# The stores of finished blocks are issued from ScalarE's queue in place of SyncE's, in a two-layer LoRA kernel on one core

## The chip, the core and the metric

The kernel runs on one core of a Trainium2 chip. The metric is the device time of one launch in microseconds (us), the median of several launches. A core has a matrix engine (TensorE, PE in the profile), three engines that work on tiles (VectorE or DVE, ScalarE or ACT, GpSimd or POOL) and SyncE (SP), which here only starts transfers. ScalarE starts some transfers too. Each engine runs its own instructions in the order in which they are written, and waits at semaphores for the others. A transfer, once issued, is carried out by 16 DMA engines, which all issuers share. The profile names SyncE's queue of transfers q1, and ScalarE's q10.

## What is computed

Two layers follow each other, each with a residual and a low-rank adapter that is picked per batch entry from a list of ids:

```python
def _L0_cond_ref(x, adapter_ids, base_weight, base_bias, lora_A_w, lora_B_w):
    result = jnp.einsum('bsd,od->bso', x, base_weight) + base_bias
    A = lora_A_w[adapter_ids]
    Bw = lora_B_w[adapter_ids]
    h = jnp.einsum('bsd,brd->bsr', x, A)
    return result + jnp.einsum('bsr,bor->bso', h, Bw)
...
def _L1_cond_ref(x, adapter_mapping, W, b, lora_As, lora_Bs):
    base_out = jnp.einsum('bti,oi->bto', x, W) + b
    A = lora_As[adapter_mapping]
    Bm = lora_Bs[adapter_mapping]
    lora_h = jnp.einsum('bti,bir->btr', x, A)
    return base_out + jnp.einsum('btr,bro->bto', lora_h, Bm) * 2
...
x = x + _L0_cond_ref(x, itok_B_6_15, ...)
x = x + _L1_cond_ref(x, itok_B_0_23, ...)
```

`x` has 8 batch entries of 512 tokens with 2048 features, float32. Both weights are 2048 x 2048, the adapters have rank 16, and there are 32 of each.

## The kernel before

The two weights are merged on the chip into one: C' (`wc_t` in HBM) is the product of the two layers' weights with their residuals, so that each token goes through one large product. The main loop has 6 planes (`pl`). Planes 0 and 1 (`pl < PRE`) make the two halves of C' out of `v_t` (the first weight, transposed) and the second weight; planes 2 to 5 take two batch entries each through C' and write `out_t`.

Each plane is one product of 2 x 2 blocks in Strassen's form: 7 products, run in the order M5, M3, M2, M4, M1, M7, M6. Four of them (M5, M2, M1, M6) need a sum or difference of two weight blocks. Each product has 16 steps; `g` counts the steps, 672 in all. A step takes one piece of weights of 128 x 512 values, `w_raw`, through these stations:

- SP loads it (`load_w`, L574), 6 steps ahead; the load waits until VectorE has finished with the piece four steps before (L571).
- For a product with a summed weight, ScalarE's queue loads the second piece, `w_second` (`load_second`, L974), 5 steps ahead, and POOL adds the two (L830). There are three buffers for `w_second`.
- ScalarE makes the high part `w_hi` (`w_split_hi`, L899), two steps ahead. It waits until TensorE has finished the step three before, since `w_hi` has three buffers (`RING`).
- VectorE makes the low part `w_lo` (L1073).
- TensorE runs 12 products of 128 x 512 (L1551 to L1553: high by high, low by high, high by low, four times).

The activations of a product go through the same split into `xop_hi` (ScalarE, L912) and `xop_lo` (VectorE, L1098), behind a sum on VectorE (L1088) where two blocks are added. After two steps an accumulator is full, and VectorE adds it into one or two blocks of the plane's result `c_out` (`evict`, L1239 and L1242); each such update counts the semaphore `c_updated` up. In planes 2 to 5 a small adapter product per accumulator goes before that (`up`; its operand `b_raw` is loaded by SP at L625 and split by ScalarE at L937). In planes 0 and 1 VectorE also adds products with the bias (`c_acc`, L1179), and adapter rows go out to HBM and back through `q_half` (SP L655 and L644, VectorE L1156).

A block of the result gets its last update in M3, M4, M7 or M6. The function `store(q, m)` then waits for that update and writes 256 KB of `c_out` out: to `wc_t` in planes 0 and 1 (L667, 64 stores), to `out_t` in planes 2 to 5 (L670, 128 stores). At step `g` those stores are issued whose evictions VectorE runs at step `g - 2`. `evictions(g)` lists them: in M7 and M6 they fall in pairs of neighbouring steps with two free steps between.

SP's program at one step is, in this order: `load_w(g + 6)`, loads of the next plane's `x_in` (L579 and L582, in M3, M7 and M6), `b_raw`, adapter rows, `q_half`, and the stores. ScalarE's is: `w_split_hi(g + 2)`, `load_second(g + 5)`, the high parts of activations, `h_split`, `b_split` and `a_split`.

Of the kernel before, what the change touches and what calls it, by code (L numbers as in the profile page):

```python
# [27 lines left out]
NPROD = len(PRODUCTS)  # L28
# [23 lines left out]
def two_layer_lora_kernel(nc, x_t, ids0, ids1, w0_t, w1_t, bias0, bias1,  # L52
# [10 lines left out]
    MH = MT // 2  # L63
# [30 lines left out]
    def upd_count(q, m, u):  # L94

        pl, i = divmod(q, NPROD)
        return pl * UPD_PASS + UPD_BASE[i] + m * N_UPD[i] + u + 1
# [20 lines left out]
    def evictions(g):  # L118

        q, j = divmod(g, STEPS)  # L120
        out = []
        for late in (1, 0):
            if 0 <= q - late < NQ:
                out += [(q - late, m) for m in EVICT.get(((q - late) % NPROD, j, late), [])]
        return out
# [98 lines left out]
    with ctx:  # L224
# [182 lines left out]
        def block_no(half, th):  # L407
            return half * 2 + th
# [18 lines left out]
        def c_diag_count(blk, m):  # L427

            return ((0, 1), (0, 0), (1, 0), (1, 1)).index(blk) * TT + m % TT + 1
# [83 lines left out]
        def columns_of(w_t, pl, th, tile):  # L513

            b = 2 * pl + th
            return w_t[TT * b:TT * b + TT, :, tile * P:(tile + 1) * P].rearrange("o p n -> p o n")

        def as_tiles(ap):
            return ap.rearrange("p (o n) -> p o n", o=TT)

        @block.sync
        def _(sp):
# [131 lines left out]
                    dst = pb_t[2 if diff else pl, :, 0:RANK, col:col + T // 2]  # L654
                sp.dma_start(dst, q_half[:, :]).then_inc(p_stored, 16)  # L655

            def store(q, m):
                pl, i = divmod(q, NPROD)
                for u, (blk, _) in enumerate(PRODUCTS[i][5]):
                    if FINAL[blk] == (i, u):  # L660
                        oh, th = blk
                        b = block_no(oh, th)
                        sp.wait_ge(c_updated, upd_count(q, m, u))
                        if pl < PRE:
                            if oh == pl and m // TT == th:
                                sp.wait_ge(c_diag_done, c_diag_count(blk, m))
                            sp.dma_start(columns_of(wc_t, pl, th, oh * MH + m), as_tiles(c_out[:, b, m, :])  # L667
                                         ).then_inc(out_stored[b], 16)
                        else:
                            sp.dma_start(out_t[2 * (pl - PRE) + th, oh * MH + m, :, :], c_out[:, b, m, :]  # L670
                                         ).then_inc(out_stored[b], 16)


            for l, ids_d in enumerate((ids0, ids1)):
                sp.dma_start(ids[0:1, l, :], ids_d.rearrange("(o n) -> o n", o=1)).then_inc(ids_loaded, 16)
# [33 lines left out]
            for g in range(NG):  # L709
                q, j = divmod(g, STEPS)  # L710
                pl, i = divmod(q, NPROD)
                s = g + 6

                for n in PARTS_AT.get(g - 1, [])[2 if g == 0 else 0:]:
                    if n + PIN < NPART:
                        load_part(n + PIN)
                    store_part(n)
                if STEPS <= s < NG:
                    load_w(s)

                if g == 0:
                    sp.wait_ge(v_stored[1], NU // 2 * 16)
                if g < 2:
                    for k in range(4 * g, 4 * g + 4):
                        load_x(0, 0, 1, k)
                if g == 2:
                    sp.dma_start(q_t[:, :], q_rows[:, :]).then_inc(small_stored, 16)
                    sp.dma_start(qd_t[:, :], qd_rows[:, :]).then_inc(small_stored, 16)
                    sp.dma_start(pb_t[2, :, RANK:R2, :], b1d_rows[:, :]).then_inc(small_stored, 16)
                if q == M1 and j < BATCH:  # L730
                    sp.dma_start(pb_t[0:2, j, RANK:R2, :].rearrange("h r n -> r h n"),
                                 lora_b1[bass.ds(adapter_of(1, j), 1), :, :].rearrange("o r (h n) -> (o r) h n", h=2)
                                 ).then_inc(b1_stored, 16)
                if g == 4:
                    sp.wait_ge(h_bias_stored, 16)
                    sp.wait_ge(h_bias_zero, 1)
                    for quad in (0, 2, 3):
                        sp.dma_start(h_bias[quad * R2 + RANK:(quad + 1) * R2, :],
                                     hb_t.rearrange("(b r) -> r b", r=RANK),
                                     allow_slow_non_contiguous=True).then_inc(h_bias_loaded, 16)  # L740
                if q == M3 and j < 2:
                    sp.wait_ge(part_filled, 2 * NPART)
                    for k in range(4 * j, 4 * j + 4):
                        load_x(0, 0, 0, k)
                if q == M3 and j == 8:
                    sp.wait_ge(ag_added, GROUPS)
                    sp.dma_start(ag_t.rearrange("b p n -> p b n"), ag[:, :, :, :].rearrange("p b k r -> p b (k r)")
                                 ).then_inc(ag_stored, 16)
                if q == M3 and 8 <= j < 12:
                    for k in range(2 * (j - 8), 2 * (j - 8) + 2):  # L750
                        load_x(0, 1, 0, k)


                if pl + 1 < NPL and i in (M7, M6) and j == 2:
                    sp.wait_ge(x_summed, n_sums(q) + KH)
                    if pl < PRE:
                        sp.wait_ge(c_scaled, (pl * 2 + (1 if i == M7 else 2)) * KT)
                if pl + 1 < NPL and i == M7 and j >= 2 and (j % 2 == 0 or j == 15):
                    load_x(pl + 1, 1, 1, (j - 1) // 2)
                if pl + 1 < NPL and i == M6:  # L760
                    for n in range(2 * KH):
                        if j == 2 + n * 14 // 16:
                            load_x(pl + 1, 0, 1 - n // KH, n % KH)
                if pl > 0 and i == M3 and j % 2 == 0:
                    load_x(pl, 1, 0, j // 2)
                for b in b_units_at(g, B_LOAD_AT):
                    load_b(*b)
                if (v := a_unit_at(g + 4)) is not None:
                    if v < PRE * 4:
                        load_a_pre(v)  # L770
                    elif v % 2 == 0:
                        load_a(v // 2)
                if (e := p_add_at(g, 1)) is not None:
                    store_p(*e)
                if (e := p_add_at(g, -2)) is not None:
                    load_q(*e)
                if g >= 2:
                    for qq, m in evictions(g - 2):
                        store(qq, m)
            for g in range(NG, NG + 4):  # L780
                for qq, m in evictions(g - 2):
                    store(qq, m)
            for qq, m in evictions(NG + 2):
                store(qq, m)
            for b in range(4):
                sp.wait_ge(out_stored[b], NPL * MH * 16)

# [46 lines left out]
        def _(act_e):  # L834
# [105 lines left out]
            def h_split_hi(pl, th):  # L940
# [4 lines left out]
                else:  # L945
# [3 lines left out]
                nc.scalar.activation(h_split[:, th, :], h_acc[:, :], ACT.Identity,  # L949
                                     bias=h_bias[:, b:b + 1]).then_inc(h_hi_ready, 1)  # L950

            def load_second(s):

                if not (STEPS <= s < NG and is_sum_w(s)):
                    return
                q, j = divmod(s, STEPS)
                pl, i = divmod(q, NPROD)
                m, h = ORDER[j]
                oh, dh = PRODUCTS[i][1][1]
                n = second_no(s)  # L960
                if s == M2 * STEPS:
                    for i_v in range(2):
                        act_e.wait_ge(v_stored[i_v], NU * 16 // 2)
                    for i_v in range(PRAW):
                        act_e.wait_ge(part_stored[i_v], NPART // PRAW * 16)
                if pl == PRE and j == 0 and i in (M5, M2):
                    for b in range(4):
                        act_e.wait_ge(out_stored[b], (PRE if i == M2 else 1) * MH * 16)
                if n >= RAW2:
                    act_e.wait_ge(w_summed, STEPS + n - RAW2 + 1)  # L970
                else:
                    act_e.wait_ge(g_turned, GROUPS)
                col = (dh * KH + h * KS) * P
                act_e.dma_start(w_second[:, n % RAW2, :], w_source(pl)[oh * MH + m, :, col:col + SW]  # L974
                                ).then_inc(wb_loaded[n % RAW2], 16)
# [50 lines left out]
            for g in range(NG):  # L1026
                q, j = divmod(g, STEPS)
                pl, i = divmod(q, NPROD)
                if g + 2 < NG:
                    w_split_hi(g + 2)  # L1030
                load_second(g + 2 + RAW2)
                for n in PART_ENDS:
                    if PART_G_AT[n] == g:
                        copy_part_g(n)
# [20 lines left out]
                    b_split_hi(*b)  # L1055
                if (v := a_unit_at(g)) is not None:
                    a_split_hi(v)

        @block.vector
        def _(dve):  # L1060
# [551 lines left out]
```

## Time and profile before

| | |
|---|---|
| time, median of 3 launches | 2151.89 us (2150.59 to 2154.97) |
| time of the profiled launch | 2147.73 us |
| its span (first to last instruction) | 2146.0 us |
| TensorE busy | 2075.3 us (97%) |
| VectorE busy | 1567.4 us (73%) |
| ScalarE busy | 737.5 us (34%) |
| GpSimd busy | 693.3 us (32%) |
| DMA queues, share of 16 engines | q1 (SP) 51.1%, q10 (ScalarE) 18.9% |
| bytes moved | 459.08 MB, mean 214 GB/s |

The profile shows one launch. Its own time is 4.2 us under the median of the three launches, and 1.7 us above its span. A busy TensorE is not the same as one at its peak, since its products are pipelined and overlap in the records. Issuing a transfer isn't counted as busy time of an engine. "Landing" is the time from a transfer's issue to its completion.

### The profile page before, as it was taken

The page shows a single profiled execution, that of the slowest core. Times are in us where ns is not written, and L with a number is a line of the kernel's source. Part 1 is how long each engine was busy: PE and PEld are TensorE (multiplying, and loading weights), DVE is VectorE, ACT ScalarE, POOL GpSimd, SP SyncE. Part 2 cuts the span into 40 slices and gives each one's busy share as a digit, 9 for nine tenths or more (in the row PEclk, how much of TensorE's full clock was granted, in tenths as well). Part 3 has the DMA queues.
Part 4 walks back from the last instruction along what each step waited for, and adds up shares of the span by engine and source line. Part 5 has one row for each costly group of instructions (what it writes and reads, how often), then busy time and mean ns, then how long its engine had stood idle before and what let it go on. Part 6 is the DMA issues. An engine that isn't in the chain of part 4 may idle for free.

```text
span 2146.0 us, 27823 instructions
## 1 busy us (share of the span) xinstructions
PE 2075.3 (97%) x9340; PEld 1710.8 (80%) x9340; DVE 1567.4 (73%) x2165; ACT 737.5 (34%) x1302; POOL 693.3 (32%) x498
## 2 busy tenths in 40 slices
PE   5799899999999999999999999999999999999999
PEld 5687787778788877888888888887888888888887
DVE  3557767977886887676876676876676876767875
ACT  5553222223322323333333333333333333333332
POOL 0222313444121445041545140544230445221443
PEclk9899999999999999999999999999999999999999
DMA  9975837796655698564698574789574789574676
GB/s 269 292 244 156 254 115 235 213 298 219 200 168 165 207 276 277 149 209 140 208 290 292 147 222 125 216 263 304 151 218 120 215 256 319 160 220 121 211 219 194
DMA packets 320122, 459.08 MB, mean 214 GB/s; under 512 B 27884, under 2 KB 131308, under 8 KB 319468
## 3 DMA queue, kind: packets, MB, share of 16 engines
q1 hardware_dynamic: 252908, 334.59, 51.1%
q10 hardware_dynamic: 67072, 122.71, 18.9%
q8 instruction: 75, 1.23, 0.2%
q14 instruction: 67, 0.55, 0.1%
HBM read 383.80 MB, written 74.45 MB: 214 GB/s over the span
## 4 chain that ended last, share of the span: by engine, by line
PE 73%; DVE 12%; DMA 8%; issue 3%; ACT 2%; SPq 1%; POOL 1%; ACTq 0%; DVEq 0%; POOLq 0%
PE acc L1551 22%; PE acc L1553 21%; PE acc L1552 21%; DVE w_lo L1073 4%; DMA w_raw<-wc_t 2%; DVE xop_lo L1098 2%; DVE c_out L1242 2%; DVE c_acc L1179 2%; PE h_acc L1463 2%; PE h_acc L1459 2%; DVE x_sum L1088 2%; DMA w_raw<-v_t 1%; PE acc L1473 1%; POOL w_raw L830 1%; DMA b_raw<-pb_t 1%
## 5 line engine op out<-in xcount | busy, mean ns | idle before, releaser
L1551 PE MATMUL acc<-xop_hi,w_hi 128*128 128x512 f32 x2688 | 1058.8, 394 | 29.8 <-DVE w_lo L1073 26.0
L830 POOL TENSOR_TENSOR w_raw<-w_raw,w_second 128x512 f32<-128x512 f32 x464 | 654.7, 1413 | 1268.5 <-DMA w_second<-wc_t 526.1
L1553 PE MATMUL acc<-xop_lo,w_hi 128*128 128x512 f32 x2688 | 1049.1, 390 | 0.0
L1552 PE MATMUL acc<-xop_hi,w_lo 128*128 128x512 f32 x2688 | 1049.0, 390 | 0.0
L1073 DVE TENSOR_TENSOR w_lo<-w_raw,w_hi 128x512 fp32r<-128x512 f32 x672 | 583.0, 871 | 406.3 <-ACT w_hi L899 402.8
L899 ACT ACTIVATE w_hi<-w_raw 128x512 fp32r<-128x512 f32 x672 | 423.9, 631 | 1181.9 <-PE acc L1553 1009.3
L1551 PEld LDWEIGHTS acc<-xop_hi,w_hi 128*128 128x128 f32 x2688 | 506.2, 188 | 151.9 <-DVE w_lo L1073 43.7
L1553 PEld LDWEIGHTS acc<-xop_lo,w_hi 128*128 128x128 f32 x2688 | 506.0, 188 | 106.2
L1552 PEld LDWEIGHTS acc<-xop_hi,w_lo 128*128 128x128 f32 x2688 | 506.4, 188 | 101.9
L1088 DVE TENSOR_TENSOR x_sum<-x_in 128x512 f32<-128x512 f32 x240 | 214.2, 904 | 0.1
L1242 DVE TENSOR_TENSOR c_out<-acc,c_out 128x512 f32<-128x512 f32 x304 | 202.2, 682 | 7.8 <-PE acc L1473 6.2
L1098 DVE TENSOR_TENSOR xop_lo<-x_sum,xop_hi 128x512 fp32r<-128x512 f32 x240 | 156.2, 682 | 4.7 <-ACT xop_hi L912 4.1
L912 ACT ACTIVATE xop_hi<-x_sum 128x512 fp32r<-128x512 f32 x240 | 135.2, 589 | 50.3 <-DVE x_sum L1088 46.8
L1098 DVE TENSOR_TENSOR xop_lo<-x_in,xop_hi 128x512 fp32r<-128x512 f32 x96 | 91.9, 990 | 0.1
L1136 DVE SCALAR_TENSOR_TENSOR b_split<-b_raw,b_split 32x128 fp32r<-32x128 f32 x128 | 51.5, 402 | 40.4 <-ACT b_split L937 37.1
L1459 PE MATMUL h_acc<-xop_hi,a_split 128*128 128x512 f32 x192 | 74.8, 390 | 0.0
L1463 PE MATMUL h_acc<-xop_lo,a_split 128*128 128x512 f32 x192 | 74.8, 389 | 0.0
L1239 DVE SCALAR_TENSOR_TENSOR c_out<-acc,c_bias,x_in 128x512 f32<-128x512 f32 x96 | 71.3, 743 | 0.0
L814 POOL TENSOR_TENSOR w_raw<-v_part 128x512 f32<-128x512 f32 x16 | 23.5, 1491 | 131.7 <-ACT v_part L873 66.6
L937 ACT ACTIVATE b_split<-b_raw 128x128 fp32r<-128x128 f32 x128 | 38.7, 302 | 73.9 <-DMA b_raw<-pb_t 72.7
L1179 DVE SCALAR_TENSOR_TENSOR c_acc<-x_in,bias,c_acc 128x512 f32<-128x512 f32 x64 | 60.1, 940 | 0.1
L912 ACT ACTIVATE xop_hi<-x_in 128x512 fp32r<-128x512 f32 x96 | 55.5, 616 | 6.0 <-DMA hb_t<-e_raw 6.0
(116 smaller groups left out, 839.4 us busy)
## 6 DMA issues: line engine op xcount, KB each, us to landing
w_raw<-wc_t SPq DMA_DIRECT2D x448, 256.0 KB, 3.8
w_second<-wc_t ACTq DMA_DIRECT2D x320, 256.0 KB, 4.4
w_raw<-v_t SPq DMA_DIRECT2D x208, 256.0 KB, 4.0
w_second<-v_t ACTq DMA_DIRECT2D x144, 256.0 KB, 4.3
x_in<-x_t SPq DMA_DIRECT2D x128, 256.0 KB, 6.1
out_t<-c_out SPq DMA_DIRECT2D x128, 256.0 KB, 5.3
x_in<-w_t SPq DMA_DIRECT2D x64, 256.0 KB, 5.6
wc_t<-c_out SPq DMA_DIRECT2D x64, 256.0 KB, 5.4
```

Of the source, the lines that this page charges most:

```text
L830: nc.gpsimd.tensor_tensor(w_raw[:, r, :], w_raw[:, r, :], w_second[:, n % RAW2, :], ALU.add if sign > 0 else ALU.subtract).then_inc(w_summ ...
L899: nc.scalar.activation(flat(w_hi[:, s % RING, :, :]), w_raw[:, r, :], ACT.Copy).then_inc(w_hi_ready, 1)
L912: nc.scalar.activation(xop_hi[:, n % XRING, :], src, ACT.Copy).then_inc(x_hi_ready, 1)
L1073: nc.vector.tensor_tensor(flat(w_lo[:, s % RING, :, :]), w_raw[:, s % RAW, :], f(flat(w_hi[:, s % RING, :, :])), ALU.subtract).then_inc(w_ ...
L1088: nc.vector.tensor_tensor(x_sum[x_bank(ns)][:, :], x_tile(q, 0, k), x_tile(q, 1, k), ALU.add if sign > 0 else ALU.subtract).then_inc(x_sum ...
L1098: nc.vector.tensor_tensor(xop_lo[:, n % XRING, :], src, f(xop_hi[:, n % XRING, :]), ALU.subtract).then_inc(x_lo_ready, 1)
L1242: nc.vector.tensor_tensor(c, bank[:, :], old, ALU.add).then_inc(c_updated, 1)
L1459: nc.tensor.matmul(h_acc[:, :], cols, xop_hi[:, n % XRING, :], start=(k == 0 and which == 0), stop=False)
L1463: mm = nc.tensor.matmul(h_acc[:, :], cols, xop_lo[:, n % XRING, :], start=False, stop=end)
L1551: nc.tensor.matmul(bank[:, :], wh, xh, start=(k == 0), stop=False)
L1552: nc.tensor.matmul(bank[:, :], wl, xh, start=False, stop=False)
L1553: mm = nc.tensor.matmul(bank[:, :], wh, xl, start=False, stop=end)
```

## The change

The function `store` moves from SyncE's block to ScalarE's, with its wait for `c_updated` (and in planes 0 and 1 for `c_diag_done`). Its calls stand on ScalarE right behind `w_split_hi(g + 2)` and `load_second(g + 5)` of the same step, ahead of everything else ScalarE does in the step. What is stored, and in which order, stays the same; SP still waits at the end for all stores.

```diff
@@ block.sync
-                if g >= 2:
-                    for qq, m in evictions(g - 2):
-                        store(qq, m)
-            for g in range(NG, NG + 4):
-                for qq, m in evictions(g - 2):
-                    store(qq, m)
-            for qq, m in evictions(NG + 2):
-                store(qq, m)
             for b in range(4):
                 sp.wait_ge(out_stored[b], NPL * MH * 16)
@@ block.scalar
+            def store(q, m):
+                pl, i = divmod(q, NPROD)
+                for u, (blk, _) in enumerate(PRODUCTS[i][5]):
+                    if FINAL[blk] == (i, u):
+                        oh, th = blk
+                        b = block_no(oh, th)
+                        act_e.wait_ge(c_updated, upd_count(q, m, u))
+                        if pl < PRE:
+                            if oh == pl and m // TT == th:
+                                act_e.wait_ge(c_diag_done, c_diag_count(blk, m))
+                            act_e.dma_start(columns_of(wc_t, pl, th, oh * MH + m), as_tiles(c_out[:, b, m, :])
+                                         ).then_inc(out_stored[b], 16)
+                        else:
+                            act_e.dma_start(out_t[2 * (pl - PRE) + th, oh * MH + m, :, :], c_out[:, b, m, :]
+                                         ).then_inc(out_stored[b], 16)
...
                 if g + 2 < NG:
                     w_split_hi(g + 2)
                 load_second(g + 2 + RAW2)
+                if g >= 2:
+                    for qq, m in evictions(g - 2):
+                        store(qq, m)
...
+            for g in range(NG, NG + 5):
+                for qq, m in evictions(g - 2):
+                    store(qq, m)
```

Three places show how the instructions now stand. The first is ScalarE's queue in M6 of plane 2, the last product of the first plane that writes outputs. Before, a high part and a second load make a step, with small splits behind them:

```order
L899 ACTIVATE w_hi<-w_raw 128x512
L974 DMA w_second<-wc_t 128x512
L937 ACTIVATE b_split<-b_raw 128x128
L899 ACTIVATE w_hi<-w_raw 128x512
L974 DMA w_second<-wc_t 128x512
L912 ACTIVATE xop_hi<-x_in 128x512
L899 ACTIVATE w_hi<-w_raw 128x512
L974 DMA w_second<-wc_t 128x512
```

In the changed kernel the same stretch reads:

```order
L875 ACTIVATE w_hi<-w_raw 128x512
L966 DMA w_second<-wc_t 128x512
L941 DMA out_t<-c_out 128x512
L913 ACTIVATE b_split<-b_raw 128x128
L875 ACTIVATE w_hi<-w_raw 128x512
L966 DMA w_second<-wc_t 128x512
L941 DMA out_t<-c_out 128x512
L888 ACTIVATE xop_hi<-x_in 128x512
L875 ACTIVATE w_hi<-w_raw 128x512
L966 DMA w_second<-wc_t 128x512
```

Two stores in neighbouring steps now stand between second loads, and ahead of the splits of `b_raw` and `x_in`.

The second place is SP's queue in the same product. Before:

```order
L574 DMA w_raw<-wc_t 128x512
L582 DMA x_in<-x_t 128x512
L625 DMA b_raw<-pb_t 128x1x128
L670 DMA out_t<-c_out 128x512
L574 DMA w_raw<-wc_t 128x512
L582 DMA x_in<-x_t 128x512
L625 DMA b_raw<-pb_t 128x1x128
L670 DMA out_t<-c_out 128x512
L574 DMA w_raw<-wc_t 128x512
L582 DMA x_in<-x_t 128x512
```

And in the changed kernel:

```order
L574 DMA w_raw<-wc_t 128x512
L582 DMA x_in<-x_t 128x512
L625 DMA b_raw<-pb_t 128x1x128
L574 DMA w_raw<-wc_t 128x512
L582 DMA x_in<-x_t 128x512
L625 DMA b_raw<-pb_t 128x1x128
L574 DMA w_raw<-wc_t 128x512
L582 DMA x_in<-x_t 128x512
```

The loads of weights, activations and `b_raw` stand as before, without the stores between them.

The third place is ScalarE's queue in M3 of plane 0, where the first four stores of the program fall. Before:

```order
L899 ACTIVATE w_hi<-w_raw 128x512 x2
L921 ACTIVATE a_split<-b_half_51 128x1024
L899 ACTIVATE w_hi<-w_raw 128x512 x3
L974 DMA w_second<-v_t 128x512
L899 ACTIVATE w_hi<-w_raw 128x512
L974 DMA w_second<-v_t 128x512
```

And in the changed kernel:

```order
L875 ACTIVATE w_hi<-w_raw 128x512 x2
L938 DMA wc_t<-c_out 128x4x128
L897 ACTIVATE a_split<-b_half_51 128x1024
L875 ACTIVATE w_hi<-w_raw 128x512
L938 DMA wc_t<-c_out 128x4x128
L875 ACTIVATE w_hi<-w_raw 128x512 x2
L966 DMA w_second<-v_t 128x512
L938 DMA wc_t<-c_out 128x4x128
L875 ACTIVATE w_hi<-w_raw 128x512
L966 DMA w_second<-v_t 128x512
```

The first two stores stand behind the high parts of steps 26 and 27, and the third behind the first load of a second piece.

## Rows read from the trace of the kernel before

**Rows 1.** Waits, whole span: who waited for whom, us, times, longest.
```profile
ACT w_hi L899 <- PE acc L1553: 1009.3, 514, 6.5
PE acc L1551 <- DVE w_lo L1073: 26.0, 24, 5.5
```

**Rows 2.** Waits of SP's queue, whole span.
```profile
SPq L574 <- DVE w_lo L1073: 1306.5, 556, 7.1
```

**Rows 3.** Instructions by line: durations of an issue in ns, min/median/max.
```profile
L974 ACTq DMA_DIRECT2D w_second<-wc_t x320: 326/326/365, 812.6 to 2125.6; - x160
L670 SPq DMA_DIRECT2D out_t<-c_out x128: 332/475/1632, 903.0 to 2143.5; - x128
L667 SPq DMA_DIRECT2D wc_t<-c_out x64: 370/438/1859, 219.4 to 838.8; - x64
```

**Rows 4.** Timeline at the longest wait for an eviction: start us, us, engine.
```profile
241.81 0.63 ACT L899 ACTIVATE w_hi<-w_raw 128x512 fp32r<-128x512 f32 x1
248.95 0.63 ACT L899 ACTIVATE w_hi<-w_raw 128x512 fp32r<-128x512 f32 x1 [6.51 <-PE acc L1553]
...
245.48 0.68 DVE L1242 TENSOR_TENSOR c_out<-acc,c_out 128x512 f32<-128x512 f32 x1
```

**Rows 5.** Timeline where high parts of activations follow the store.
```profile
584.69 1.14 ACT L912 ACTIVATE xop_hi<-x_in 128x512 fp32r<-128x512 f32 x2
586.87 0.63 ACT L899 ACTIVATE w_hi<-w_raw 128x512 fp32r<-128x512 f32 x1 [1.04 <-PE acc L1553]
...
585.74 0.68 DVE L1242 TENSOR_TENSOR c_out<-acc,c_out 128x512 f32<-128x512 f32 x1
```

**Rows 6.** Timeline of TensorE behind two of its longest waits.
```profile
243.74 0.79 PE L1551 MATMUL acc<-xop_hi,w_hi 128*128 128x512 f32 x1 [5.47 <-DVE w_lo L1073]
...
1469.15 0.50 PE L1551 MATMUL acc<-xop_hi,w_hi 128*128 128x512 f32 x1 [1.51 <-DVE w_lo L1073]
```

**Rows 7.** Chain that ended last, 205 to 250 us: start us, us, what.
```profile
228.15 6.51 DMA pb_t<-q_half
...
234.68 4.36 DMA q_half<-qd_t
```

**Rows 8.** Stretches: length, busy us (instructions) of PE PEld DVE ACT POOL, PEclk, DMA share, GB/s.
```profile
214.00:217.00 3.00, 3.00 (x15) 2.49 (x14) 3.00 (x5) 0.00 (x0) 0.00 (x0) 1.00 0.48 131
...
223.00:226.00 3.00, 3.00 (x15) 2.50 (x14) 3.00 (x6) 0.63 (x1) 0.00 (x0) 1.00 1.10 315
...
244.00:248.00 4.00, 4.00 (x10) 3.13 (x11) 3.97 (x7) 0.00 (x0) 1.13 (x1) 0.50 0.62 181
```

**Rows 9.** Timeline of DVE, ACT and SP around the first store.
```profile
211.90 0.68 DVE L1242 TENSOR_TENSOR c_out<-acc,c_out 128x512 f32<-128x512 f32 x1
...
213.02 0.63 ACT L899 ACTIVATE w_hi<-w_raw 128x512 fp32r<-128x512 f32 x1 [2.37 <-PE acc L1553]
...
219.44 1.47 SPq L667 DMA_DIRECT2D wc_t<-c_out  x1
```

**Rows 10.** Stretch in M6 of plane 2, columns as in rows 8.
```profile
1117.00:1160.00 43.00, 42.89 (x189) 35.21 (x189) 26.70 (x36) 16.02 (x31) 19.89 (x15) 1.00 0.99 335
```

**Rows 11.** Landings of `w_second` (L974) issued 1117 to 1163 us.
```profile
DMA to landing us min/median/max: 3.3/6.0/7.5
```

**Rows 12.** Landings of `w_raw` (L574) issued 1117 to 1163 us.
```profile
DMA to landing us min/median/max: 3.9/7.1/9.7
```

**Rows 13.** Landings of `out_t` (L670) issued 1117 to 1163 us.
```profile
DMA to landing us min/median/max: 6.3/6.7/9.0
```

**Rows 14.** Waits in 1117 to 1163 us.
```profile
ACT w_hi L899 <- POOL w_raw L830: 13.5, 7, 2.6
POOL w_raw L830 <- DMA w_raw<-wc_t: 13.3, 7, 3.5
...
POOL w_raw L830 <- DMA w_second<-wc_t: 9.8, 6, 2.8
```

More of the change, by code:

```diff
@@ L655, in store_p @@
                 sp.dma_start(dst, q_half[:, :]).then_inc(p_stored, 16)
[L657 to L671, printed above, removed]
             for l, ids_d in enumerate((ids0, ids1)):
```

## The prediction

> **What bounds the kernel now.** I read four views, from the whole to the place. First the waits of the whole span: ScalarE waits 1009.3 us for TensorE, and TensorE waits 26.0 us, in 24 pieces, for low parts of weights [rows 1]. With TensorE busy in 97% of the span, TensorE is the bound, and what any change of queues can give back is those 26.0 us and what they cost in clock. Second, SP's own waits: it stands 1306.5 us before loads of `w_raw`, waiting for VectorE [rows 2]. SP's queue is thus far from full on the average, and its time is worth something only in stretches where it falls behind. Third, the longest of TensorE's waits: 5.47 us at 243.74 us, in M3 to M2 of plane 0, and as an example of the others 1.51 us at 1469.15 us [rows 6]. Fourth, the DMA share by stretch: it is 1.10 around 225 us and 0.99 in M6 of plane 2, where the loads for the next plane run [rows 8, 10]. There the DMA engines are the scarce thing, and an issuer can only change the order in which they are used.
>
> **What the change takes from SP.** The 192 issues have medians of 475 ns (128 of them) and 438 ns (64) [rows 3]: 128 x 0.475 + 64 x 0.438 = 89 us leave SP's queue. SP has 1306.5 us of waiting to set against that, so outside the saturated stretches the gain is 0. `w_raw` is issued when VectorE releases it, with or without stores in front.
>
> **What it adds to ScalarE: issue time.** An issue of `w_second` takes ScalarE's queue 326 ns [rows 3]. The nearest row for a store there is that one from below and SP's 475 ns from above, so 63 to 91 us go into a queue that waits 1009.3 us for TensorE. Cost 0. The cover would be gone only where ScalarE has no wait before its next high part. I take the lower value, since SP's longer issues stand in stretches where its own queue of transfers is full.
>
> **What it adds to ScalarE: a wait.** The store of step g waits for an eviction that VectorE makes in its step g - 2. Behind it on ScalarE stand the step's high parts of activations, `b_split`, `a_split`, and the next step's high part of weights and load of a second piece. The worst place is in M3 of plane 0: the high part starts at 241.81 us and ends at 242.44, the eviction ends at 245.48 + 0.68 = 246.16 us, and the next high part starts only at 248.95 us, behind TensorE [rows 4]. The wait of 3.7 us fits into that gap with 2.8 us to spare. The worst place with work right behind is in M3 of plane 1: two high parts of activations start at 584.69, the first update ends at 585.74 + 0.68 = 586.42 [rows 5]. They start 586.42 + 0.33 - 584.69 = 2.1 us late, take 1.14 us, and move the next high part from 586.87 to about 587.9, by 1.0 us. VectorE needs none of these before it has done its steps g - 1 and g, since the eviction waited for belongs to g - 2. Where VectorE is late enough to make ScalarE wait, it is also late in asking for ScalarE's work. Cost 0. From above: the few places with such work right behind, three of this kind at 1.0 us, give 3 us.
>
> **M3 of plane 0.** This is the dearest wait of the kernel. TensorE stands 5.47 us [rows 6], and afterwards runs at a granted clock of 0.50, that is 1.2 in place of 2.4 GHz: 10 products in 4.00 us [rows 8], where 43.00 / 189 = 0.2275 us each [rows 10] would give 17.6. That is 7.6 x 0.2275 = 1.7 us more, 7.2 us in all. The chain to it goes through SP's queue: `q_half` is stored at 228.15 us, lands 6.51 us later, is loaded again at 234.68 and lands after 4.36 us [rows 7]. In this stretch SP issues without a pause, the store at 219.44 takes it 1.47 us [rows 9], and the first two stores of C' stand ahead of the adapter row. Is that row now earlier? The first store can go much sooner. Its eviction ends at 211.90 + 0.68 = 212.58 us, ScalarE's high part ends at 213.65, so it goes at about 213.7 in place of 219.44 [rows 9], into a stretch with a DMA share of 0.48 [rows 8]. But the third and fourth are also no longer held back by SP, and fall into the stretch with share 1.10, beside the row that matters. About as many bytes as before come before it. I take 0. From below the whole 7.2 us come back; from above one store more ahead costs what one issue under back-pressure took, 1.5 us, with its share of slow clock 2 us.
>
> **M6 of planes 0 to 4.** Here second pieces are loaded for M6 and M5, the next plane's activations come in, and stores follow in pairs. A store of 256 KB is now in the queue of `w_second`, between two of them. In M6 of plane 2 `w_second` lands in 6.0 us, `w_raw` in 7.1, `out_t` in 6.7 (medians) [rows 11, 12, 13]. POOL waits for `w_raw` 7 times (13.3 us) and for `w_second` 6 times (9.8 us), and ScalarE 13.5 us for POOL [rows 14]: both are at the edge. There is a ring: the high part of step s is made beside the issue of the second piece of s + 3, so a landing that grows by d makes each third step later by d. If `w_second` lands like the stores, d = 0.7, and 16 steps give 0.7 x 16 / 3 = 3.7 us. The lead of ScalarE over TensorE is two steps, 2 x 12 x 0.2275 = 5.5 us; less a high part of 0.63 [rows 4] and about as much for the low part, 4.1 us are left to eat. So TensorE pays 0 at d = 0.7. `w_raw`, without stores in its queue, may be sooner by as much, on the 7 waits that it ends. I take 0.2 us for each of the five, +1 us, since the lead is not whole when M6 begins. Bounds: -1 (POOL's waits for `w_raw` shorten) and +1.8 each (below).
>
> The Trainium skill speaks against a gain here: its page "DMA: Bandwidth & Descriptors", section "Issuing engines are not separate DMA queues", says that transfers started by several engines run on the same 16 DMA engines and interleave, so that only the issue time is saved. The trace agrees in part: in the saturated stretch both queues are slow, 6.0 and 7.1 us, though not alike. By the rule alone the sum would be 0 in place of +1.
>
> **The end.** The last stores go out from one idle queue in place of another: 0.
>
> **The sum.** 0 + 0 + 0 + 0 + 1 + 0 = +1 us on 2147.7 us for the profiled launch. That launch is 4.2 us under the median of the three, so on the median I have 2151.9 + 1 = 2153 us. Within 0.2% (4.3 us) is about what a measurement of this kernel can't tell from no change.
>
> **The rivals.**
>
> *The stall in M3 goes* (faster). If the early first store and the shorter SP queue bring the adapter row forward, VectorE isn't held and 7.2 us come back; `w_raw` and `b_raw` sooner in M6 would take the wait at 1469.15 us too, 1.5 us. Together 8.7: 2143 us. For it: SP's issue of 1.47 us shows a queue of transfers that is full. Against: DMA shares of 1.10 leave nothing to win by order except for who comes first. Chance 0.22.
>
> *Second pieces come late* (slower). It decides from d = 4.1 x 3 / 16 = 0.8 us on. If `w_second` becomes as slow as `w_raw` now is, d = 7.1 - 6.0 = 1.1, 16 steps give 5.9 us, less 4.1 of lead 1.8 us in each of five planes, 9 us: 2161 us. For it: in M6 the issues of `w_second` are already close to the point where POOL waits. Against: the DMA engines' total work is the same, and a later product pulls its loads apart. Chance 0.26. A rule of the Trainium skill would bring this about: the same page, section "Queues, rings and completion order", has each DMA engine take turns between the rows of its queues, packet by packet. A short queue would then keep its turn only as long as it is short, and each store delays the second piece behind it. No row here shows the turns themselves.
>
> *ScalarE's wait isn't hidden* (slower). The three places of M3 with high parts behind the store pay in full, 3 us, and a wait of TensorE of 5.47 us has shown that the clock then adds a third: +4 and the +1 of above, 2157 us. Against: the ordering argument above. Chance 0.06.
>
> *No part of it shows*: the likeliest, with its own range 2148 to 2156. Chance 0.46.
>
> **How the numbers follow.** The predicted time is that of the likeliest case, 2153 us. Faster 0.22 is the first rival, slower 0.32 the second and third. The range of 2144 to 2163 us reaches to the fast rival's better half and takes in most of the slow one.
>
> **What would show it.** Right: DMA issues of `w_second` near 0.33 us with stores beside them; SP's wait before `w_raw` longer by some 80 us; TensorE's wait for low parts near 26 us in all; a wait near 243 us of 4 to 7 us. In M6 `w_second` should land in 6.5 to 7 us and `w_raw` in 6 to 7. Wrong: no half-clock stretch near 245 us (the fast rival), POOL's waits for `w_second` well up and TensorE waiting in M6 of planes 2 to 4 (the slow one), or high parts that start right behind an eviction with TensorE waiting (the third).

## The result

The changed kernel takes 2155.12 us (median of 20 launches, 2144.24 to 2166.27), the kernel before 2148.26 us (20 launches, 2139.57 to 2154.97). The ratio is 1.0033, with a 95% interval of 1.002 to 1.0046. It is slower by 0.33%, some 7 us; the forecast was 2153 us, with "No part of it shows" as the likeliest case. The measured time lies in the stated range, but the loss came by a way that none of the rivals named.

The profiled launch of the changed kernel took 2163.83 us and is near the top of its spread, while that of the kernel before lies at its median. So of the 16 us between the two profiles less than half is the change. Page of the changed kernel, its DMA queues, and who waited for whom (us in total, times, longest):

```profile
q1 hardware_dynamic: 200684, 284.25, 43.9%
q10 hardware_dynamic: 119296, 173.06, 25.8%
```

```profile
ACT w_hi L875 <- PE acc L1551: 930.9, 477, 5.8
...
ACT b_split L913 <- DMA b_raw<-pb_t: 110.7, 57, 5.4
...
PE acc L1549 <- DVE w_lo L1071: 38.6, 25, 5.0
```

SP's own waits:

```profile
SPq L574 <- DVE w_lo L1071: 1435.0, 583, 8.7
```

Seven percent of the DMA engines' time went from SyncE's queue to ScalarE's. SP stands 128 us longer before its loads of `w_raw` (1306.5 us before [rows 2]), more than the 89 us of issues that left it. ScalarE waits less for TensorE (1009.3 us before [rows 1]), and TensorE more for low parts, 38.6 in place of 26.0 us. The row for which the prediction has no term is the second: ScalarE waits 110.7 us for `b_raw`, which the prediction names only in its fast rival, as coming sooner. In the kernel before that row reads:

```profile
ACT b_split L937 <- DMA b_raw<-pb_t: 72.7, 51, 4.0
```

TensorE's longest wait in the changed kernel is still the one near 244 us, 4.97 us. The next three (start us, us) stand in M6 of planes 2, 3 and 4, where the longest of the kernel before is the 1.51 us at 1469.15 us [rows 6]:

```profile
1142.05 0.50 PE L1549 MATMUL acc<-xop_hi,w_hi 128*128 128x512 f32 x1 [4.29 <-DVE w_lo L1071]
...
1476.24 0.50 PE L1549 MATMUL acc<-xop_hi,w_hi 128*128 128x512 f32 x1 [4.01 <-DVE w_lo L1071]
...
1811.76 0.58 PE L1549 MATMUL acc<-xop_hi,w_hi 128*128 128x512 f32 x1 [3.48 <-DVE w_lo L1071]
```

The chain of work that TensorE waited for (start us, us), led back from the third of them, holds four loads of `b_raw`, 35 of its last 54 us:

```profile
1757.55 10.20 DMA b_raw<-pb_t
...
1770.51 8.64 DMA b_raw<-pb_t
...
1785.66 5.72 DMA b_raw<-pb_t
...
1795.44 10.42 DMA b_raw<-pb_t
...
1805.88 0.32 ACT b_split L913
...
1806.55 1.43 DVE a_raw L1112
1808.00 0.43 DVE a_raw L1115
...
1810.43 0.68 DVE c_out L1240
1811.11 0.61 DVE w_lo L1071
```

Each load waits until VectorE has split an earlier one, since `b_raw` has two buffers. ScalarE's timeline shows what stands behind such a split:

```profile
1800.30 0.63 ACT L875 ACTIVATE w_hi<-w_raw 128x512 fp32r<-128x512 f32 x1 [2.27 <-POOL w_raw L806]
...
1805.88 0.31 ACT L913 ACTIVATE b_split<-b_raw 128x128 fp32r<-128x128 f32 x1 [4.95 <-DMA b_raw<-pb_t]
1808.54 0.63 ACT L905 ACTIVATE a_split<-a_raw 128x512 fp32r<-128x512 f32 x1 [2.34 <-DVE a_raw L1115]
...
1809.59 0.61 ACT L875 ACTIVATE w_hi<-w_raw 128x512 fp32r<-128x512 f32 x1
```

The next high part of weights is written behind the split, and comes 9.3 us after the last one, where a step is 2.7 us long. The late load makes 4.95 us of that. Most of the rest is other work of the same step: it is step 8 of M6, in which VectorE also sums the adapter operand `a_raw` behind its part of `b_split`, and ScalarE splits it (`a_split`) ahead of the next high part. VectorE then has its part of `a_split`, an eviction and the low part to do. The waits of 4.29 and 4.01 us have the same chain behind them, with loads of `b_raw` of 9.06 and 9.93 us and the same `a_split`. So a late `b_raw` hurts most where this second split stands behind it; no run moved `a_split`. The two steps of lead are gone, TensorE waits 3.48 us, and then runs slowly for a while (stretch, busy us and instructions of PE PEld DVE ACT POOL, granted clock, DMA share, GB/s):

```profile
1812.00:1815.00 3.00, 3.00 (x8) 2.34 (x8) 2.97 (x4) 0.21 (x1) 1.40 (x1) 0.51 0.93 240
```

The granted clock is 0.51, the lower of its two levels (1.2 GHz). Eight products in 3.00 us, where 0.2275 us each would give 13, cost 1.2 us more.

The profiled launch is a slow one, but e1 and e5 below, profiled at 2154.22 and 2155.47 us, close to their medians, have such waits in M6 of planes 2, 3 and 4 too: 2.60, 4.15 and 2.66 us in e1, 2.86, 1.03 and 4.23 us in e5.

### The profile page after: what moved, and what is told of

Its sections match the earlier page's. It is cut to its first block, busy times and chain, and to the rows that moved or that the text cites. A ratio compares the mean times of both kernels' runs of the same rounds, so it can differ in the third digit from the quotient of the medians.

```text
span 2162.1 us, 27823 instructions
## 1 busy us (share of the span) xinstructions
PE 2078.3 (96%) x9340; PEld 1714.2 (79%) x9340; DVE 1574.9 (73%) x2165; ACT 740.7 (34%) x1302; POOL 690.3 (32%) x498
## 4 chain that ended last, share of the span: by engine, by line
PE 74%; DVE 11%; DMA 8%; issue 3%; ACT 1%; SPq 1%; POOL 1%; ACTq 0%; DVEq 0%; POOLq 0%
PE acc L1549 22%; PE acc L1551 22%; PE acc L1550 22%; DVE w_lo L1071 3%; DMA b_raw<-pb_t 3%; PE h_acc L1461 2%; PE h_acc L1457 2%; DVE c_out L1240 2%; DVE xop_lo L1096 2%; DVE x_sum L1086 2%; DVE c_acc L1177 1%; DMA w_raw<-v_t 1%; PE acc L1471 1%; DMA v_t<-v_raw 1%; DMA q_half<-pd_t 1%
## 5 line engine op out<-in xcount | busy, mean ns | idle before, releaser
L1549 PE MATMUL acc<-xop_hi,w_hi 128*128 128x512 f32 x2688 | 1059.0, 394 | 42.1 <-DVE w_lo L1071 38.6
L1071 DVE TENSOR_TENSOR w_lo<-w_raw,w_hi 128x512 fp32r<-128x512 f32 x672 | 589.3, 880 | 380.5 <-ACT w_hi L875 377.2
L1086 DVE TENSOR_TENSOR x_sum<-x_in 128x512 f32<-128x512 f32 x240 | 222.6, 939 | 0.1
L1096 DVE TENSOR_TENSOR xop_lo<-x_in,xop_hi 128x512 fp32r<-128x512 f32 x96 | 82.7, 892 | 2.3 <-ACT xop_hi L888 2.1
L913 ACT ACTIVATE b_split<-b_raw 128x128 fp32r<-128x128 f32 x128 | 39.0, 305 | 118.4 <-DMA b_raw<-pb_t 110.7
```

The source lines that it names most:

```text
L1071: nc.vector.tensor_tensor(flat(w_lo[:, s % RING, :, :]), w_raw[:, s % RAW, :], f(flat(w_hi[:, s % RING, :, :])), ALU.subtract).then_inc(w_ ...
L1086: nc.vector.tensor_tensor(x_sum[x_bank(ns)][:, :], x_tile(q, 0, k), x_tile(q, 1, k), ALU.add if sign > 0 else ALU.subtract).then_inc(x_sum ...
L1096: nc.vector.tensor_tensor(xop_lo[:, n % XRING, :], src, f(xop_hi[:, n % XRING, :]), ALU.subtract).then_inc(x_lo_ready, 1)
L1549: nc.tensor.matmul(bank[:, :], wh, xh, start=(k == 0), stop=False)
```

## The experiments

Three theories were set against each other. **T**: transfers. Stores that no longer stand behind SyncE's loads are carried out ahead of them, SyncE's loads land later, and `b_raw` with its two buffers is the one that TensorE feels. **R1**: ScalarE's order. ScalarE stands at stores whose eviction isn't done. **R2**: weights. `w_second` or `w_raw` lands late, and POOL is the one that is waited for (the slow rival of the prediction). Each kernel was timed against the kernel before in five rounds, with 12 launches (the changed kernel 20); all ratios are to the kernel before as timed beside it. The last column is from the one profiled launch of each, and TensorE feels only part of it.

| kernel | ratio | 95% interval | median us | wait of ScalarE for `b_raw`, us |
|---|---|---|---|---|
| changed kernel | 1.0033 | 1.002 to 1.0046 | 2155.12 | 110.7 |
| e1: only M7 and M6 moved | 1.003 | 1.0011 to 1.005 | 2156.12 | 99.3 |
| e2: only M3 and M4 moved | 1.0002 | 0.9989 to 1.0015 | 2151.73 | 90.9 |
| e3: changed, `b_raw` early | 0.9976 | 0.9958 to 0.9995 | 2146.31 | 26.5 |
| e4: before, `b_raw` early | 1.0003 | 0.9988 to 1.0018 | 2150.69 | 21.6 |
| e5: changed, stores two steps later | 1.0027 | 1.001 to 1.0044 | 2155.42 | 70.8 |
| e6: changed, `b_raw` on ScalarE | 0.9994 | 0.997 to 1.0018 | 2149.01 | 4.1 |
| e7: changed, `b_raw` first in the step | 1.0008 | 0.9989 to 1.0028 | 2151.22 | 9.3 |
| e8: e3, adapter rows first | 0.9968 | 0.9949 to 0.9987 | 2143.18 | 19.0 |
| e9: before, stores first in the step | 1.0023 | 1.0008 to 1.0037 | 2152.86 | 80.7 |
| e10: e4, adapter rows first | 0.9998 | 0.9981 to 1.0015 | 2146.92 | 21.9 |
| e11: e8, stores one step later | 0.9995 | 0.9981 to 1.0009 | 2146.65 | 28.4 |
| e12: e3 again | 0.9975 | 0.9959 to 0.9991 | 2143.78 | 18.9 |

### Where: e1 and e2

```diff
 # ScalarE, behind load_second; SyncE issues the others as before
                 if g >= 2:
                     for qq, m in evictions(g - 2):
+                        if qq % NPROD in (M7, M6):     # e2: (M3, M4)
                         store(qq, m)
```

Expected of e1: 

> Only the stores of M7 and M6 are issued by ScalarE, those of M3 and M4 by SyncE as before. Theory (T): the loss comes where stores and the next plane's loads share the DMA engines, and the stores now overtake SyncE's loads of weights and b_raw. Then this kernel loses all of the 0.33%: 2154 to 2157 us against 2148. Rival (R1): ScalarE's wait for late evictions costs, wherever the eviction is late, above all behind M3 and M4, where it ends after the high part at most planes. Then this kernel loses a third or less: within 3 us of before.

Expected of e2: 

> Only the stores of M3 and M4 are issued by ScalarE. (T): no load of activations runs there in planes 2 to 5, so it is as before, within 3 us of 2148, and the wait of 5.5 us in M3 of plane 0 may be a little shorter. (R1): most of the 7 us is lost here.

e1 loses what the whole change loses (1.003), e2 nothing (1.0002). The loss is made by the stores of M7 and M6, where the next plane's activations are loaded. R1, which had the late evictions behind M3 and M4, fails its first test. e2's wait for `b_raw` of 90.9 us in its profiled launch warns that this sum alone does not set the time: what counts is where the waits stand.

### What carries it: e3, e4 and e12

```diff
-M7: (-3, -2, 1, 2, 5, 6, 9, 10)}          # B_LOAD_AT
+M7: (-4, -3, -1, 0, 3, 5, 7, 9)}
+        def b_buf(bu):
+            return ident[:, :] if bu % 3 == 2 else b_raw[:, bu % 3, :]
...
-                if bu >= 2:
-                    sp.wait_ge(b_lo_ready, bu - 1)
-                sp.dma_start(b_raw[:, bu % 2, :],
...
+                if bu >= 3:
+                    sp.wait_ge(b_lo_ready, bu - 2)
+                sp.dma_start(b_buf(bu),
```

Expected of e3: 

> The changed kernel with a third buffer for b_raw, and its loads for M7 and M6 one or two steps earlier. (T) with b_raw as the carrier of the loss: ScalarE's wait for b_raw falls from 110.7 us to under 40, TensorE's waits of 3.5 to 4.3 us in M6 of planes 2 to 4 go, and the time falls by 5 to 12 us against the changed kernel, to 2144 to 2150. Rival (R2): weights are the carrier, w_raw lands late and POOL waits for it; then the waits in M6 stay, and the time is within 3 us of 2155.

Expected of e4: 

> The kernel before with the same third buffer and the same earlier loads of b_raw: the control of the run above. (T): ScalarE waits 72.7 us for b_raw before, and little of it reaches TensorE, so 0 to 5 us faster than 2148; the gap between the two stores' places shrinks from 7 us to under 3. (R2): gap of 7 us as before.

Expected of e12: 

> The changed kernel with the third buffer of b_raw and its earlier loads, the same kernel as e3, run again beside fresh runs of the kernel before. It was 0.9976 (0.9958 to 0.9995), and a near relative with stores one step later was 0.9995. If the gain over the kernel before is real, the ratio is again 0.995 to 0.999 and clear of 1; if it was the luck of one chip and hour, it is within 0.1% of 1. Either way it should stay clear of the changed kernel's 1.0033.

The third buffer is `ident`, an identity matrix that isn't read any more in planes 2 to 5. With a third buffer and earlier loads the changed kernel loses its 0.33% and is faster than the kernel before, 0.9976, and 0.9975 when run again. The same edit on the kernel before is worth nothing (1.0003). R2 is out as the carrier of this loss: if POOL's waits for weights had made the loss, a third `b_raw` would not have taken it away. The waits in M6 of plane 4, first those of the changed kernel (1762 to 1821 us), then those of e3 (1748 to 1802 us):

```profile
POOL w_raw L806 <- DMA w_raw<-wc_t: 24.0, 12, 4.3
ACT b_split L913 <- DMA b_raw<-pb_t: 20.8, 7, 5.2
DVE b_split L1134 <- ACT b_split L913: 14.4, 6, 4.6
...
PE acc L1549 <- DVE w_lo L1071: 5.2, 3, 3.5
```

```profile
POOL w_raw L813 <- DMA w_raw<-wc_t: 19.2, 10, 3.6
...
PE acc L1556 <- DVE w_lo L1078: 0.4, 1, 0.4
```

The waits for `b_raw` are gone and TensorE's with them, though POOL still waits 19.2 us for `w_raw`: those waits are hidden. The two launches compared are a slow and a fast one (2163.83 and 2141.12 us), so the times above, and not these rows, carry the argument. The edit gives a buffer and moves loads at once; which of the two does it wasn't tested. I had expected the gap between the two places of the stores to shrink; it turned round, which the theory didn't foresee.

### Not ScalarE's order: e5

```diff
-                if g >= 2:
-                    for qq, m in evictions(g - 2):
+                if g >= 4:
+                    for qq, m in evictions(g - 4):
                         store(qq, m)
```

Expected of e5: 

> The changed kernel with its stores issued four steps behind the eviction in place of two, so that ScalarE never waits for an eviction; nothing else moves. Theory (T): the loss comes from transfers, since stores in a queue of their own are served beside SyncE's loads and hold b_raw up. Later stores hold it up as much: 2152 to 2158 us against 2149 to 2152. Rival (R1): ScalarE stands at stores whose eviction isn't done, and what is behind it (b_split, high parts) comes late. Then the whole loss goes: within 2 us of before.

With two steps more between eviction and store, ScalarE's waits that end with VectorE's updates of `c_out` fall from 13.6 to 5.2 us, and the kernel stays as slow as it was (1.0027). R1 is out. The sum of the waits for `b_raw` is as low as 70.8 us here, yet TensorE still waits 4.2 us at once in M6 of plane 4, and the rows there read (1757 to 1815 us):

```profile
ACT b_split L913 <- DMA b_raw<-pb_t: 11.1, 4, 3.5
PE acc L1549 <- DVE w_lo L1071: 4.2, 1, 4.2
```

### Order in the queues: e6, e7 and e9

```diff
 # e7, SyncE
+                for b in b_units_at(g, B_LOAD_AT):
+                    load_b(*b)
                 if STEPS <= s < NG:
                     load_w(s)
...
-                for b in b_units_at(g, B_LOAD_AT):
-                    load_b(*b)
```

e6 has the same two lines on ScalarE, between `load_second` and the stores. e9 is the kernel before with the stores at that place in SyncE's step.

Expected of e6: 

> The changed kernel with the loads of b_raw on ScalarE's queue too, behind the loads of second pieces and ahead of the stores; two buffers, same steps. (T): b_raw leaves the queue that holds w_raw and x_in, lands in 5 to 6 us in place of 7 to 8 in M7 and M6, and the loss is gone or turned: 2144 to 2150 us. (R1): the order of ScalarE's work gets longer by 128 issues and waits, so 2155 us or more. If b_raw lands no sooner, turn-taking between the queues isn't what held it up.

Expected of e7: 

> The changed kernel with SyncE's loads of b_raw ahead of the weights and activations of the same step, still in SyncE's queue. (T): two transfers of 256 KB no longer stand ahead of b_raw, each worth 0.7 to 1.3 us, so it lands 1.5 to 2.5 us sooner and most of the loss goes: 2146 to 2152 us. (R2, weights as carrier): no change, 2155 us.

Expected of e9: 

> The kernel before, all in SyncE's queue, with the stores at the head of SyncE's step, ahead of the weights, activations and b_raw of the same step. If what costs is that a store is served ahead of b_raw, in whatever queue, then the loss shows without any second queue: ScalarE's wait for b_raw rises from 72.7 us to 90 or more, and the time is 2152 to 2156 us against 2149. If it takes a second queue to overtake (turns between queues), one store of 0.7 us more ahead of b_raw is not enough: within 2 us of before, and the wait for b_raw under 85 us.

Putting `b_raw` ahead of two transfers of the same step takes the wait for it from 110.7 to 9.3 us, and most of the loss by the median (1.0008, though the interval reaches 1.0028). The small waits don't mean fast landings. In M6 of planes 2 to 4 TensorE still waits 1.84, 1.49 and 2.26 us, each at the step with `a_split`, and the chain of the last one holds this load:

```profile
1786.45 8.96 DMA b_raw<-pb_t
```

On ScalarE's queue the loss is gone as well (0.9994). There I had the reason wrong: `b_raw` doesn't land in 5 to 6 us, and one load issued at 1778.81 us is still waited for when its split starts at 1789.10 us. In that stretch stores and second pieces took up to 12 us in place of 7, so the queue of ScalarE was now the slower one, as the landings of `w_second` in M6 of plane 4 show (1750 to 1805 us):

```profile
DMA to landing us min/median/max: 4.1/6.1/12.2
```

The second piece that took longest, 12.15 us from 1784.98 us, stands in the chain of a wait of TensorE of 2.18 us: in this order the weights do reach TensorE.

e6 recovers the time because ScalarE issues the load sooner in its step, or because SyncE's queue is lighter; the run doesn't say which.

e9 asks whether it takes a second queue at all. The time says no: with all stores in SyncE's queue, but ahead of the loads of their step, the kernel before loses 0.23%. But its wait for `b_raw`, 80.7 us, stayed below 85 us, where 90 or more was expected if the loss came through `b_raw`, and TensorE's waits in M6 of its profiled launch are short. So that stores issued ahead of SyncE's loads of the same step cost time is measured; that they do so through `b_raw` in e9 too is not.

### Toward a faster version: e8, e10 and e11

```diff
 # e8 and e10, SyncE
+                if (e := p_add_at(g, 1)) is not None:
+                    store_p(*e)
                 if STEPS <= s < NG:
                     load_w(s)
...
-                if (e := p_add_at(g, 1)) is not None:
-                    store_p(*e)
```

Expected of e8: 

> The kernel with the changed stores and the third buffer of b_raw, and the adapter rows stored ahead of the weights and activations of the same SyncE step. In M3 of plane 0 the wait of TensorE near 244 us is 5 to 6 us in all kernels so far, and hangs on such a row. If its place in SyncE's step decides, 2 to 5 us of that wait go, and the time is 2142 to 2145 us; if the saturated DMA engines decide, it is as with the third buffer alone, 2146.

Expected of e10: 

> The stores in SyncE's queue as before, with the third buffer of b_raw and adapter rows ahead of weights. The control of the fastest version so far (0.9968). If the stores' place is worth something once b_raw doesn't hang on it, this one is slower than that by 3 to 7 us: 2147 to 2151 us. If only b_raw and the rows count, it is as fast, 2142 to 2145.

Expected of e11: 

> The fastest version so far with stores three steps behind the eviction in place of two. If ScalarE's waits for evictions cost something in it (its high parts wait 3.2 us for evictions in all), 1 to 3 us come back: 2140 to 2143 us. If they cost nothing, it is the same, ratio 0.995 to 0.998.

e8 is the fastest, 0.9968, but its interval holds e3's ratio. TensorE's wait near 244 us is 6.30 us in e3, 4.27 in e8 and 4.04 in e10:

```profile
245.75 0.79 PE L1556 MATMUL acc<-xop_hi,w_hi 128*128 128x512 f32 x1 [6.30 <-DVE w_lo L1078]
```

```profile
245.60 0.79 PE L1556 MATMUL acc<-xop_hi,w_hi 128*128 128x512 f32 x1 [4.27 <-DVE w_lo L1078]
```

```profile
243.94 0.79 PE L1558 MATMUL acc<-xop_hi,w_hi 128*128 128x512 f32 x1 [4.04 <-DVE w_lo L1080]
```

That the row's place in the step does this isn't shown: e12, the same kernel as e3, waits 5.21 us there, and e11, which has the row in front as e8 has, 5.88 us. e10 with both edits and the stores in SyncE's queue is at 0.9998, so against e8 the stores' place is worth about 0.3% once `b_raw` doesn't hang on it. e11, with the stores a step later, was to give 1 to 3 us and lost most of the gain (0.9995), so that it is no better than e10; why isn't settled.

## Why the prediction was right and wrong

That the measured time lies in the likeliest case's own range, 2148 to 2156 us, is luck as far as the mechanism goes: the term that carries the loss isn't in the sum.

**What bounds the kernel.** Right: TensorE is the bound, and most of what the change added to its waits stands in stretches in which the DMA engines are nearly full (a share of 0.87 to 0.92 in M6 of planes 2 to 4). One more, 2.73 us at 2071.90 us in plane 5, does not: VectorE is busy there for 11.94 of 12 us, with a DMA share of 0.65. Whether the change made it isn't known.

**SyncE's issues, ScalarE's issues.** Right in cost. Issues of `out_t` on ScalarE took 0.44 us (median), between the two bounds. e3 keeps all of them and is faster than the kernel before, so they cost nothing that the time shows. SP's wait grew by 128 us, where some 80 were forecast.

**ScalarE's wait for evictions.** Right at 0: e5 takes most of it away and gains nothing, and e2 has the places with the longest waits and loses nothing.

**M3 of plane 0.** Right at about 0. The first store goes at 214.07 us, against 213.7 forecast. The adapter row goes at 227.42 us and lands after 8.00 us, where it took 6.51 us from 228.15 [rows 7], and TensorE waits 4.97 us in place of 5.47 [rows 6], but 1.41 us more at 253.57 us, where the kernel before waits 0.30. The chain of the changed kernel there:

```profile
227.42 8.00 DMA pb_t<-q_half
...
235.44 4.42 DMA q_half<-qd_t
```

ScalarE's timeline with the early store:

```profile
214.07 0.42 ACTq L938 DMA_DIRECT2D wc_t<-c_out  x1
```

**M6 of planes 0 to 4.** Here a step failed: the term of +1 us. The text says of the SyncE side that "`w_raw`, without stores in its queue, may be sooner", and puts the cost on `w_second`, which was to land like the stores, 0.7 us later. For the stores and `w_raw` it was the other way round. In M6 of plane 4 the landings of `out_t`, `w_raw` and `w_second` in the changed kernel, in that order (issued 1762 to 1821 us):

```profile
DMA to landing us min/median/max: 3.5/5.7/7.4
```

```profile
DMA to landing us min/median/max: 4.0/7.5/9.5
```

```profile
DMA to landing us min/median/max: 3.7/5.5/7.2
```

The kernel before has medians of 6.8, 6.8 and 6.4 us there. In planes 2 and 3 the medians of `out_t` went from 7.2 and 6.8 to 5.7 and 5.7 us, and those of `w_raw` from 7.2 and 6.3 to 7.6 and 7.2. So in all three planes stores land 1.1 to 1.5 us sooner, and SyncE's loads of weights 0.4 to 0.9 us later. `w_second` has no such direction: 0.4 us sooner, 0.4 later, 0.9 sooner. The signs that the prediction gave for itself, 6.5 to 7 us for `w_second`, 6 to 7 for `w_raw` and 26 us of waits of TensorE, all failed, and its sign of being wrong, TensorE waiting in M6 of planes 2 to 4, came. The prediction followed `w_raw` and `w_second`, and gave `b_raw` no term. `b_raw` has less slack than the weights, which are loaded 6 and 5 steps ahead: its load stands 3 steps, about 8.2 us, ahead of its split, its two buffers allow hardly more, and the split stands ahead of the next high part in ScalarE's queue. Landings of 8.6 to 10.4 us are over that. In planes 2 to 4 that made waits of 4.29, 4.01 and 3.48 us for TensorE, with the `a_split` of the same step in the chain. It is 12 us in a launch from the slow end, against +1 us forecast for the term; the whole loss at the median is 7 us.

**The rivals.** The fast one didn't come. "Second pieces come late" had the sign and the stretch right, and the wrong transfer: its condition d of 0.8 us never held for `w_second`. Its rule, taken from the Trainium skill (page "DMA: Bandwidth & Descriptors", section "Queues, rings and completion order"), that the DMA engines take turns between queues, would fit the landings of stores and `w_raw` above, with stores in a short queue served sooner than at the end of a long one. I drew from it the delay of what is in the short queue, and not the one of what is left in the long queue. No run shows the turns, and e9 lost time with one queue. The rule of the Trainium skill (the same page), section "Issuing engines are not separate DMA queues", by which only issue time is saved, missed the 0.3%: which transfer is carried out first was worth more than the issues.

## What to carry over

To move transfers to another queue is to reorder transfers where the DMA engines are full. List every load of that stretch with its slack in time to its use and its number of buffers; the smallest and rarest one may decide. In one queue, a transfer that nobody waits for did better behind the loads of its step than ahead of them (e9). Before it goes to another queue, give the loads that it will overtake another buffer or an earlier issue (e3). An in-order engine that splits a small operand ahead of a large one passes the small one's lateness on to the matrix engine, above all in a step that has other small work behind it.

## What the runs showed beyond that

Once `b_raw` has three buffers and earlier loads, stores in ScalarE's queue are better than in SyncE's (0.9976 and 0.9975 against 1.0003), though in M6 of plane 4 of e3 they still land sooner than `w_raw` (6.8 against 7.4 us, medians). Which load or wait gains from that wasn't found, and e11, with the same queues and the stores one step later, doesn't have the gain (0.9995). The granted clock fell to its lower level behind a wait of 3.48 us as it does behind one of 5.47 us (0.51 and 0.50 [rows 8]), and these two waits of TensorE cost about a third more than they last. Behind the wait of 1.51 us at 1469.15 us it stayed at 1.00 (1469 to 1473 us), so no slow stretch followed that one.
